# Cross attention and an RWKV layer: statistics moved to ScalarE, two sums moved into transfers, another order of the passes

## The reference

```python
# stage 1, cross attention, per batch
g_x   = einsum('oc,bct->bto', Wg, x) + bg
theta = einsum('oc,bct->bot', Wtheta, x) + btheta
phi   = einsum('oc,bct->bot', Wphi, ctx) + bphi
y     = softmax(phi^T theta) @ g_x                  # 256 x 256 scores
w_y   = einsum('oc,btc->bot', Wz, y) + bz
w_y   = gamma * (w_y - mean) * rsqrt(var + EPS) + beta   # over batch and t, per channel
x     = w_y + x                                     # called z below
# stage 2, RWKV layer; 64 tokens a batch, width 256, 32 heads of 8
xn  = layernorm(x);  sx = shifted(xn) - xn
xxx = tanh((xn + sx*maa_x) @ maa_w1); five mixes x5[j] = xn + sx*(stack[j] + xxx[j] @ maa_w2[j])
w = exp(-exp(time_decay + tanh(x5[1] @ decay_w1) @ decay_w2))
r, k, v, g = x5[3] @ Wr.T, x5[0] @ Wk.T, x5[2] @ Wv.T, silu(x5[4] @ Wg.T)
per token: out = r (u * k v + s);  s = k v + w * s  # scan over 64 tokens, state 8 x 8 a head
x1  = x + (groupnorm(out) * g) @ Wo.T
xn2 = layernorm(x1); sx2 = shifted(xn2) - xn2; xk, xr = xn2 + sx2*ffn_maa_k, xn2 + sx2*ffn_maa_r
out = x1 + sigmoid(xr @ Wr2.T) * (relu(xk @ Wk2.T)^2 @ Wv2.T)
```

## Time and profile before

| what | value |
|---|---|
| median of 3 runs | 730.25 us |
| the profiled execution | 732.31 us, its span 730.5 us |
| granted TensorE clock, mean | 0.965 of full speed |
| busy: TensorE, VectorE, ScalarE, GpSimd | 635.5, 637.0, 362.0, 262.1 us |
| attention, with its last statistics | to about 172 us |
| first scan | at 221.29 us |
| moved by transfers | 54.18 MB |

### The profile page before, as it was taken

One profiled execution on the slowest core, in us unless ns is written; L12 is line 12 of the kernel. 1 busy time (PEld: TensorE's weight loads), 2 busy tenths in 40 slices (PEclk: granted clock), 3 DMA queues, 4 the chain that ended last, 5 costly groups with the idle time before them and its releaser, 6 DMA issues.

```text
span 730.5 us, 9667 instructions
## 1 busy us (share of the span) xinstructions
PE 635.5 (87%) x2704; PEld 351.7 (48%) x2704; DVE 637.0 (87%) x1001; ACT 362.0 (50%) x799; POOL 262.1 (36%) x189
## 2 busy tenths in 40 slices
PE   7789999997996778999889899989988989995796
PEld 5466666665542223444435445344443534533365
DVE  2489999995467999999999999999999999979954
ACT  3468888882233317245444644625554472451343
POOL 1850000000002765636337355453733536452000
PEclk9689999999998997999999999999999999998799
DMA  2711222220066056053432705515161360560000
GB/s 64 217 45 57 57 59 63 64 59 3 28 132 127 1 115 144 1 115 79 95 64 51 172 0 115 131 41 114 55 119 40 75 144 0 115 133 12 0 30 29
DMA packets 38332, 54.18 MB, mean 74 GB/s; under 512 B 4643, under 2 KB 21187, under 8 KB 38179
## 3 DMA queue, kind: packets, MB, share of 16 engines
q1 hardware_dynamic: 36882, 50.46, 31.1%
q0 software_dynamic: 1424, 3.43, 1.5%
HBM read 16.13 MB, written 4.19 MB: 28 GB/s over the span
## 4 chain that ended last, share of the span: by engine, by line
DVE 31%; PE 18%; issue 16%; POOL 4%; ACT 3%; DMA 2%; SPq 1%; DVEq 1%; ACTq 0%; POOLq 0%
DVE state L1423 13%; PE ps_a L794 4%; PE ps_a L823 3%; DVE x L1386 3%; PE ps_c L880 2%; DMA vb<-v 2%; POOL state L685 2%; DVE state L1410 2%; PE ps_a L806 2%; DVE st L1354 2%; POOL x L690 1%; DVE sx L1520 1%; SPq L630 1%; DVE sx L1501 1%; PE ps_att L860 1%
## 5 line engine op out<-in xcount | busy, mean ns | idle before, releaser
L690 POOL TENSOR_TENSOR x<-x,xn 128x1024 f32<-128x1024 f32 x35 | 87.5, 2502 | 199.2 <-DVE x L1386 199.2
L1423 DVE TENSOR_TENSOR_SCAN state<-ps_w,state 128x512 f32<-128x512 f32 x128 | 145.8, 1200 | 0.7
L794 PE MATMUL ps_a<-x,wsq 128*128 128x512 f32 x256 | 118.2, 602 | 5.9 <-ACT xn L1124 3.0
L685 POOL TENSOR_TENSOR state<-vb,k 128x2016 f32<-128x2016 f32 x23 | 107.3, 4664 | 23.7 <-DMA vb<-v 15.6
L1428 DVE TENSOR_TENSOR vb<-state,r 128x2048 f32<-128x2048 f32 x32 | 96.6, 3018 | 1.7
L794 PEld LDWEIGHTS ps_a<-x,wsq 128*128 128x128 f32 x256 | 47.5, 192 | 65.9 <-issue 52.3
L823 PE MATMUL ps_a<-mix_t,w 128*128 128x512 f32 x128 | 62.5, 610 | 15.6 <-DVE x L1386 9.6
L1386 DVE SCALAR_TENSOR_TENSOR x<-ps_a,vec,sx 128x512 f32<-128x512 f32 x80 | 57.2, 744 | 13.3 <-PE ps_a L823 12.0
L296 ACT ACTIVATE probs<-ps_f,negmax 128x256 f32<-128x256 f32 x128 | 59.1, 473 | 2.0 <-DVE negmax L345 1.2
L345 DVE TENSOR_REDUCE negmax<-ps_f 128x2 f32<-128x512 f32 x64 | 41.2, 686 | 7.9 <-PE ps_f L218 5.5
L823 PEld LDWEIGHTS ps_a<-mix_t,w 128*128 128x128 f32 x128 | 22.5, 189 | 50.8 <-DVE x L1386 17.3
(11 more groups left out here) (203 smaller groups left out, 1233.7 us busy)
## 6 DMA issues: line engine op xcount, KB each, us to landing
vb<-v SPq DMA_DIRECT2D x128, 256.0 KB, 5.8
x<-in_x SPq DMA_DIRECT2D x32, 128.0 KB, 2.1
c<-in_ctx SPq DMA_DIRECT2D x32, 128.0 KB, 2.1
x_chunk<-in_x SPq DMA_DIRECT2D x8, 512.0 KB, 7.4
out<-sx SPq DMA_DIRECT2D x7, 512.0 KB, 3.5
wsq<-in_wsq POOLq DMA_DIRECT2D x1, 1024.0 KB, 5.4
wsq<-in_wsq POOLq DMA_DIRECT2D x1, 768.0 KB, 6.9
s<-in_s POOLq DMA_DIRECT2D x1, 512.0 KB, 7.9
```

Of the source, the lines that this page charges most:

```text
L685: nc.gpsimd.tensor_tensor(st[q][:, :, :, 1:L], src[:, :, :, 0:L - 1], wide(k[p][h][:, :])[:, :, :, 0:L - 1], ALU.mult).then_inc(kv_at(n, h ...
L690: nc.gpsimd.tensor_tensor(x5[j % 2][:, :, :], x5[j % 2][:, :, :], xn[:, :, 1:L1], ALU.add).then_inc(x5_ready, 1)
L794: mm = nc.tensor.matmul(bank[:, :], wsq[:, weight, c, P * o:P * o + P], src(c), start=(c == 0), stop=(c == EC - 1))
L1423: nc.vector.tensor_tensor_scan(row, w[h][:, :], row, 0.0, ALU.mult, ALU.add).then_inc(scanned, 1)
```

## The change

1. **Attention start.** The six small weights are fetched on ScalarE's queue; SP fetches the theta and phi weights right after the first pair, and the second pair ahead of the identity. TensorE does proj(0), then the combined weights (in the transposes' banks), scores(0), then values(0) and proj(1).
2. **Paced fetches.** Each late weight (some cut in two or seven pieces) waits for a pair of its own to have landed.
3. **Score banks.** Three rotating ones, and one attend bank for both pairs. Loops run six pairs a turn.
4. **Bridge.** `norm_params` is dissolved into `rwkv`; the first z takes x without bnb, its bias is added later on ScalarE.
5. **z by transfer.** ScalarE makes wyz*bna + bnb in place, and a transfer issued by GpSimd adds x from memory to it (`z_add`).
6. **Statistics of the first layer norm** for chunks 1 to 7 go to ScalarE (`a_zs`): sums by a copy with accumulator, then squares of deviations.
7. **The last sum.** SP stores x1 to the output as soon as it is there; a transfer issued by GpSimd adds the gated value y to it in memory (`add_out`). `c_final` goes. The factor 0.5 is folded into the weight FV.
8. **Mixes two at a time.** `w2` sits in two halves of 64 rows, so that the matmuls of two mixes use different rows of TensorE and different banks. VectorE's `a_mod` goes half by half over two mixes.
9. **Order of the passes** on all engines; the first spread of v goes out in two halves.

```diff
@@ attention
-        ps_f, ps_t, ps_av = [pb("ps_f0"), pb("ps_f1")], [...], [pb("ps_av0"), pb("ps_av1")]
+        ps_f, ps_t, ps_av = [pb(f"ps_f{i}") for i in range(3)], [...], pb("ps_av")
+        def score_bank(k, e):
+            return ps_f[(2 * k + e) % 3]
@@ gpsimd
-            pool.wait_ge(s_xin[1], 64)
+            def after_pair(pi):
+                pool.wait_ge(s_xin[pi % 2], 32 * (pi // 2 + 1))
...
+                after_pair(max(3, i + 1))
                 pool.dma_start(...).then_inc(t["s_late"], 16)
@@ tensor
-                wait(pe, s_exp, pi * 2)
+                wait(pe, s_exp, pi * 2 - 1)
...
-                wait(pe, s_wy, pi - 1)
+                wait(pe, s_wy, pi)
@@ rwkv, gpsimd
+            def z_add(n):
+                pool.wait_ge(x_biased, n)
+                pool.dma_start(wyz[:, bass.ds(n * TILES, TILES), :], d["x"][...], accum_op=ALU.add).then_inc(z_ready, 16)
+            def add_out(n):
+                pool.wait_ge(y_mid, n * 2 + 4)
+                pool.wait_ge(x1_stored, n * 16 + 16)
+                pool.dma_start(out[...], y, accum_op=ALU.add).then_inc(stored, 16)
@@ body, gpsimd
+                prev(n - 1, sx2_ready, xprev2, t["prev0"], xn2)
                 b_kv(n, p, 0, 1)
                 prev(n + 1, sx_ready, xprev, t["prev1"], xn)
                 add_x(n + 1, 0)
                 b_kv(n, p, 1, 0)
+                if z:
+                    z_add(n + 2)
                 add_x(n + 1, 1)
-                prev(n - 1, sx2_ready, xprev2, t["prev0"], xn2)
                 rstd(n - 1, ...); add_x(n + 1, 2); add_x(n + 1, 3); rstd(n + 2, ...)
                 b_kv(n + 1, q, 0, 0)
                 add_x(n + 1, 4)
+                add_out(n - 1)
@@ body, tensor
-                a_mod(n + 1, 0)
-                c_out(n - 1)
-                a_mod(n + 1, 1)
+                a_mod_pair(n + 1, 0, 0, 1)
+                a_mod_pair(n + 1, 1, 0, 1)
+                b_reduce(n, 0, 0)
+                c_out(n - 1)
                 a_dec1(n + 1)
...
                 a_proj(n + 1, 2, "k", WK)
-                c_value(n - 1)
-                a_mod(n + 1, 4)
                 b_reduce(n, 1, 0)
+                a_mod_last(n + 1)
                 b_reduce(n, 1, 1)
+                c_value(n - 1)
                 a_proj(n + 1, 3, "r", WR)
@@ body, scalar
+            def a_zs(n):
+                act.wait_ge(z_ready, n * 16)
+                for m in range(TILES):
+                    nc.scalar.activation(zn[...], wyz[...], ACT.Copy, accum_out=row_sum[:, m:m + 1])
+                act.wait_ge(row_sums1, (n - 1) * TILES + TILES)
+                nc.scalar.activation(ve1[:, 1, :], row_sum[:, :], ACT.Copy, scale=-1.0 / E)
+                deviations(n, ve1, zn, ...)      # four ACT.Square with bias -mean and accum_out
...
                 c_kk(n - 1)
+                if z:
+                    a_zs(n + 2)
                 a_copy(n + 1, "k", k[q], k_ready)
                 c_rr(n - 1)
@@ body, vector (whole order after)
+                b_scan(n, p, 0, 0); b_ruk(n, p); a_shift(n + 1); b_bonus(n, 0); b_bonus(n, 1); c_gn(n - 1, q)
+                a_mod(n + 1, 0, 0, 1); a_mod(n + 1, 1, 0, 1); b_scan(n, p, 0, 1); c_x1(n - 1)
+                b_scan(n, p, 1, 0); c_shift(n - 1); a_mod(n + 1, 0, 2, 3); b_kv(n, p, 1, 1)
+                a_mod(n + 1, 1, 2, 3); b_scan(n, p, 1, 1); a_mod(n + 1, 0, 4); a_mod(n + 1, 1, 4)
+                c_gate_value(n - 1)
-                c_final(n - 1)
@@ sync
-            def store(n):
-                sp.wait_ge(out_ready, n * 2 + 2)
+            def store_x1(n):
+                sp.wait_ge(x1_ready, n * 2 + 2)
+                sp.wait_ge(stored, n * 16 + 16)
```

More of the change, by code:

```diff
@@ L32 @@
 L1 = L + 1
-LATE = 32
+LATE = 37
 HH = H // 2
@@ L144, in _ @@
         def _(pool):
-            for m, value in ((ones, 1.0), (bd_th, 0.0), (bd_ph, 0.0), (bd_gz, 0.0)):
+            for m, value in ((bd_th, 0.0), (bd_ph, 0.0), (ones, 1.0), (bd_gz, 0.0)):
                 nc.gpsimd.memset(m[:, :], value).then_inc(s_zero, 1)
@@ L511, in rwkv @@
               "r0": (r_ready, 1, 2), "r1": (r_ready, 2, 2), "g0": (gate_ready, 1, 2), "g1": (gate_ready, 2, 2)}
-    for j in range(5):
-        A_READ[f"w{j}a"], A_READ[f"w{j}b"] = (mod_ready, 2 * j + 1, 10), (mod_ready, 2 * j + 2, 10)
+    MOD_ORDER = ["w0a", "w1a", "w0b", "w1b", "w2a", "w3a", "w2b", "w3b", "w4a", "w4b"]
+    for at, name in enumerate(MOD_ORDER):
+        A_READ[name] = (mod_ready, at + 1, 10)
     NA, NA_COUNT = len(A_ORDER), len(A_COUNT)
@@ L628, in spread_v @@
                 wait(sp, prod_used, n * 4 + 2 * h - 2)
+                if h == 0 and isinstance(n, int) and n == 0:
+                    for q, landed in ((0, v_first), (1, v_spread[0])):
+                        for i in range(S):
+                            sp.dma_start(vb[0][i:P:S, q:S:2, :], v[0][q:P:2, :]).then_inc(landed, 16)
+                    return
                 for i in range(S):
                     sp.dma_start(vb[h][i:P:S, :, :], v[h][:, :]).then_inc(v_spread[h], 16)
-            def store(n):
-                sp.wait_ge(out_ready, n * 2 + 2)
-                sp.dma_start(out[bass.ds(n * TILES, TILES)].rearrange("a p f -> p a f"), y).then_inc(stored, 16)
+            def store_x1(n):
+                sp.wait_ge(x1_ready, n * 2 + 2)
+                sp.wait_ge(stored, n * 16 + 16)
+                sp.dma_start(out[bass.ds(n * TILES, TILES)].rearrange("a p f -> p a f"), wyz[:, bass.ds(n * TILES, TILES), :]).then_inc(x1_stored, 16)
             def store_last(i):
@@ L748, in _ @@
             first_pass(0, 0)
+            pool.wait_ge(stored, 16)
             with pool.Fori(1, CHUNKS - 4, 2) as n:
@@ L1081, in drain_pass @@
                 last_values(1)
+            half = cst[:, HALF, :]
+            pe.wait_ge(t["s_late"], 16 * LATE)
+            warm(WARM_A)
+            pe.wait_ge(s_loc, 1)
+            nc.tensor.matmul(abank[0][:, 0:2], half, mv[:, 0:2], start=True, stop=True).then_inc(s_mean, 1)
+            warm(WARM_B)
+            pe.wait_ge(s_dev, 4)
+            nc.tensor.matmul(abank[1][:, 0:2], half, mv[:, 4:6], start=True, stop=True).then_inc(s_var, 1)
             warm(WARM_D)
@@ L1360, in moments @@
                 nc.vector.tensor_scalar(veb[:, 1, :], mvb[:, :, 0], -1.0, None, ALU.mult).then_inc(s_var, 1)
-            def a_z(n):
-                dve.wait_ge(x_biased, n + 1)
-                z = wyz[:, bass.ds(n * TILES, TILES), :]
-                nc.vector.scalar_tensor_tensor(z, z, t["bna"][:, 0:1], xr_in[:, :, :], ALU.mult, ALU.add).then_inc(z_ready, 1)
             def a_zm(n):
-                moments(n, z_ready, n + 1, st1b, mv1, ve1, st1, mv1_s, ln1_var)
+                first = isinstance(n, int) and n == 0
+                moments(n, z0_ready if first else z_ready, 1 if first else n * 16, st1b, mv1, ve1, st1, mv1_s, ln1_var)
             def a_shift(n):
```

498 lines of the change are left out of this document (253 added, 245 removed).

## The result

The changed kernel took 700.45 us (median of 4; 697.98 to 701.44), the kernel before, run beside it, 730.16: ratio 0.9588, 95% interval 0.9562 to 0.9615. The forecast was 677 with a range of 662 to 697. The sign was right; of 54.5 us forecast, some 30 came. The profiled execution took 699.89 us with a span of 698.0, so on the spans 730.5 became 698.0, 32.5 us less.

The account below looks back on a forecast made before the run. Bound taken as stage by stage: waits on fetches, then ScalarE's exponentials in attention, VectorE in the passes. Gains summed to 54.5 us, giving 677.8 from 732.31 or 675.8 from the 730.25 median; forecast 677, range 662 to 697.

Parts of the forecast that it names:

- the signs that I had named for being wrong: Pairs staying at 4.46 us, idle before the gate value absent or over 4 us, or ScalarE waiting for z's transfer.
- Attention start, pacing, banks, bridge: Attention and bridge: earlier start -3.3, paced fetches -8, three score banks -6.7, bridge to the first z -3.3 us.
- Chain now: k copies near 211, spread near 213: -5: Pipeline fill: v and its half spread go out earlier, saving 5 us, with bounds of 2 and 7.
- First pass: -4: First pass: loses z, moments and a locked last product, gains a scan waiting for GpSimd; 4 us less.
- And that stays hidden: VectorE is the bound: Steady passes: TensorE's saving of some 2 us from 64-row matmul pairs brings no time, as VectorE sets the pass.
- The locks, +1.2 a pass: Steady passes: VectorE and GpSimd locking each other out costs 2.5 (half hidden), 1.5 and 0.5 us, thus 1.2 more.
- Last pass and drain: End of the kernel: spread limited only by the last reduction, -4 us; last sum off the critical line, -1.2.
- The last sum: Drain: VectorE's final addition leaves the critical line, saving 1.2 us.
- the second pass: Second pass, 66.5 us before: the state product now runs beside the scan, saving 6 us.
- Rival 2: Transfers from GpSimd start late, held by VectorE's locked products; 2.3 us over 6 passes, 691 us in all; chance 0.07.
- Rival 1: Passes give nothing back: gate wait and locks take all 6.7 us, passes stay near 61; 693 us; chance 0.15.
- Rival 4: Slower than before: z's adding transfer lands late and ScalarE's sums wait for it; 737 us at 28 us landing; chance 0.03.

Follow-up runs that it names:

- kv_first: Changed kernel with VectorE's first state product and first scan of the fill ahead of the last modulation; 704.56 us, ratio 0.9673 to the kernel before.
- fill2: first_free plus, in the fill, GpSimd's first state product waiting for VectorE's additions and nine warm-up matmuls ahead of k; 692.93 us.
- first_free: Changed kernel with the fill's first product ahead of the last modulation, and GpSimd's first-pass state product (h 1, q 0) waiting for VectorE's product; 696.64 us.
- red_early: Changed kernel with reduction (h 1, q 0) moved ahead of the channel mix's keys, and ScalarE's attention-sum copy ahead of its decay exponentials; 695.37 us.
- kv01_early: Changed kernel with GpSimd's next-pass state product (h 0, q 1) ahead of the output's adding transfer, two previous-column copies swapped; 696.68 us.
- moments_dve: Changed kernel with the layer norm's moments of z back on VectorE instead of ScalarE's sums; 707.16 us, ratio 0.9675 to the kernel before.
- best1: first_free combined with kv01_early; 695.26 us, ratio 0.9516 to the kernel before the change.
- best2: fill2 plus the moves of kv01_early and the early reduction of red_early; 684.92 us, ratio 0.9367 to the kernel before the change.
- best3: best2 plus the value product of the channel mix ahead of the last reduction on TensorE; 685.88 us, ratio 0.9400 to the kernel before the change.

## Why the prediction was wrong

The mechanism of the attention part held; what failed are steps in the fill, the first pass and the end of a steady pass (points 2, 3 and 4). Of the signs that I had named for being wrong none appeared clearly: pairs are 4.2 us apart, the two waits for the value product sum to 3.2 us (4.15 with the one for the mix), and ScalarE did not wait for the transfer of z. They watched neither the fill nor the first pass.

1. *Attention start, pacing, banks, bridge:* right in sum (22.65 for 21.3). The first maxima came at 12.13, not 10.4; pacing made that good (21.8 us for five intervals, forecast 24). The 26 later intervals gained 4.4 of 6.7 us, since some 2 us of GpSimd's preparation now lie in them, which the forecast had booked under pacing. The bridge gave its 3.3.
2. *"Chain now: k copies near 211, spread near 213: -5"* failed. I followed the spread, which did land early, and let k stand. k hangs on mixes 2 and 3, which the new order puts behind v; its copy came 35.5 us after bna, 34.8 before. Behind it, in VectorE's order, stood a mix that comes after k. kv_first shows how much hangs on that order: the scan came 6.3 us sooner (1.3 of it the clock), nearly the 7.0 missing, but the first pass paid more than that. fill2, which keeps the scan behind the mix, gets 2.8 us. The last 4.2 us no kernel here has brought in without a loss elsewhere.
3. *"First pass: -4"* failed on a lock that I had not laid out for this pass. first_free shows 4.6 us, the whole miss of 4.3: the product of 7.15 us fell to 2.29.
4. *"And that stays hidden: VectorE is the bound"* is the step that failed in the steady passes. VectorE's removed work was right (6.65 us, of which 0.5 went back into locks). But TensorE's row ends the pass. I counted a reduction and half a value product, 2.8 us against 1.35 of modulation, and took the modulation's own input as there. It comes from the same row: 0.94 us of wait. The last reduction, which I let start when VectorE's product ended (488.62), started at 490.31 behind that modulation, and the value product with it. So the pass ended 7.1 us after the product and not 5.2; the waits sum to 4.15 us, forecast 2.5. red_early, which takes one reduction out, gives 1.35 us a pass; kv01_early, which takes 2.2 us off VectorE at the head of the pass, gives 0.25. In its second half moments_dve shows that VectorE's time still counts (1.9 of 2.35).
5. *The locks, +1.2 a pass:* they measured 2.2 and 1.4 us where I had 2.5, 1.5 and 0.5, so VectorE's busy time grew by 0.5 and not by 1.2. My own terms do not give 1.2 either: 4.5 less 3.12 is 1.4, and with half of the first hidden 0.1. And kv01_early shows that the first lock costs almost nothing. This error went the other way; without it the miss would have been larger.
6. *Last pass and drain:* the scan (0, 1) came 16.65 us into the pass instead of 19.5, 2.9 of the 4 us. The last sum was no longer worth 1.2: an attend product stood behind it. The rest is in part TensorE's slower keys: the last pass and the drain took 81.7 to 82.4 us in four profiles in which the clock did not fall there (kv01_early, moments_dve, best1, best2) and 83.4 here. Why the clock fell I did not test. Nor did I test the second pass apart, so its 2.9 us stay open: in best3 it took 58.1 us.
7. *Rival 2* (transfers from GpSimd start late) is refuted: every issue took 1.29 to 1.37 us, also the one at 461.85, which lay beside VectorE's product (460.39 to 464.06), and the adding transfer of z landed in 5.7 to 6.0 us.

```profile
461.85 1.30 POOL L662 DMA_DIRECT2D wyz<-in_x  x1
```

"SBUF — State Buffer", section "SBUF: two separate sides", in the Trainium skill, says that such an issue starves while VectorE holds the pair, measured beside a copy; beside the two-input products of this kernel no run shows it. Its other half, that the lock is exclusive, agrees to the tenth of a microsecond, as the last section shows. *Rival 1* (693) was the nearest in size. Its reason, VectorE's last operations waiting for a TensorE that is busy 56 of 61.6 us, is the right one for the steady passes, but they gave back 1.95 us each and did not stay near 61; 17.8 of the 22 us missing lie in other stages. That its total is near is in good part luck. *Rival 4* is out: the sums on ScalarE began at 480.98, long after the transfer issued at 461.85 had landed. Its sum has a slip: 10 us a pass over seven passes are 70, and 747, not 737.

## What to carry to other kernels

When work is taken off the busiest engine, lay out the last ten microseconds of the loop on all engines before you book the gain: here the next bound was there as a row without gaps. Follow each input of a waiting instruction, not only the one that was late before. A lock between two engines is priced by what stands behind it: 2.2 us cost 0.25 here in one place and, in another, 4.9 us cost 4.6. Look at the granted clock of both profiles before a gain of one or two microseconds is put down to an edit: eight matmuls of the fill took 5.40 us in some profiles of the same order and 3.70 in others. Moving an instruction up into idle time is only a gain if what it releases does not run into the next.

## What the hardware showed

The lock is for whole instructions. A VectorE product that begins while GpSimd's state product runs lasts until that one ends, and then its own 2.2 us:

| product starts | GpSimd ends | sum with 2.2 | product ended |
|---|---|---|---|
| 222.71 | 227.70 | 229.90 | 229.86 |
| 257.92 | 261.70 | 263.90 | 263.85 |
| 440.84 | 443.20 | 445.40 | 445.36 |

In the first row the product began first by 0.03 us, and GpSimd still went first; so it was in eight profiles, by 0.01 to 0.03 us. With a lead of 0.19 us the product kept the lock: it took its 2.29 us, and GpSimd's state product, 4.5 alone, took 6.45.

```profile
605.14 2.29 DVE L1460 TENSOR_TENSOR vb<-state,r 128x2048 f32<-128x2048 f32 x1
```
```profile
605.33 6.45 POOL L656 TENSOR_TENSOR state<-vb,k 128x2016 f32<-128x2016 f32 x1 [0.96 <-issue]
```

Likewise a GpSimd operation on 128x4 values, 0.20 us alone, took 2.06 us behind a product that had begun 0.3 us before it. GpSimd's issue of an adding 512 KB transfer took 1.3 us; it landed in 5.8 us into SBUF, and in 9.3 us (median) into HBM. The last figure is not the transfer's own: in kv01_early, best1 and best2, where it is issued behind the state product and not ahead of it, the medians were 6.3, 6.4 and 6.1. Which neighbour costs the 3 us is open. Four 64-row matmul records, two at a time, took 1.13 us where four of 128 rows took 1.88 to 2.01.
